# A graph network in one kernel: other program order for the first six units of its edge layer, and a last unit that ends on VectorE and ScalarE

## What is computed

```python
def _L3_gnn_ref(x, adj, W1, b1, W2, b2, gamma, beta):
    hi = jnp.einsum('bsh,hk->bsk', x, W1[:H])
    hj = jnp.einsum('bsh,hk->bsk', x, W1[H:])
    h = jax.nn.relu(hi[:, :, None, :] + hj[:, None, :, :] + b1)
    y = jnp.einsum('bijk,kl->bijl', h, W2) + b2
    y = _layernorm(y, gamma, beta)
    out = jnp.einsum('bij,bijh->bih', adj, y)
    return out
x = _layernorm(x + _L0_gnn_ref(x, adj, nodemask, ...), axis=-1)
x = _layernorm(x + _L1_gnn_ref(x, adj, adj, ...), axis=-1)
x = _layernorm(x + _L2_gnn_ref(x, adj, ...), axis=-1)
x = _layernorm(x + _L3_gnn_ref(x, adj, ...), axis=-1)
```

## Time and profile before

| | us |
|---|---|
| median of 3 runs | 465.38 (464.74 to 468.73) |
| the profiled execution | 467.42 |
| its span, first to last instruction | 465.7 |
| mean granted PE clock in it | 0.984 of full speed |
| PE busy in it | 435.3 (93%) |
| DVE, ACT, POOL busy | 411.8, 386.6, 357.8 |

### The profile page before, as it was taken

How to read it: one execution, slowest core, us unless ns; L and a number is a source line. 1 busy time by engine, 2 the same in 40 slices (tenths; PEclk the granted TensorE clock), 3 DMA queues, 4 the chain that set the end, 5 groups by cost and what they waited for, 6 DMA issues and landing times. The chain is left out here.

```text
span 465.7 us, 14118 instructions
## 1 busy us (share of the span) xinstructions
PE 435.3 (93%) x3394; PEld 414.4 (89%) x3427; DVE 411.8 (88%) x1518; ACT 386.6 (83%) x994; POOL 357.8 (77%) x656
## 2 busy tenths in 40 slices
PE   3799989999999999789999999999999999999980
PEld 2699989999999999679999999999999999999980
DVE  5799999999999999947998898899889888989873
ACT  2368979999999899787788888888888888989872
POOL 4379989998999898816777777777778776878745
PEclk9989999999999999899999999999999999999996
DMA  6134345545445652243322222222222231213111
GB/s 218 40 82 126 101 141 165 158 130 179 146 146 181 204 175 82 85 121 96 104 73 76 81 71 81 69 83 67 85 66 86 64 88 62 90 62 87 34 36 47
DMA packets 50939, 47.60 MB, mean 102 GB/s; under 512 B 5584, under 2 KB 42576, under 8 KB 50896
## 3 DMA queue, kind: packets, MB, share of 16 engines
q1 hardware_dynamic: 49600, 46.29, 32.5%
q10 hardware_dynamic: 1296, 0.83, 0.6%
HBM read 28.22 MB, written 18.87 MB: 101 GB/s over the span
## 5 line engine op out<-in xcount | busy, mean ns | idle before, releaser
L1420 PEld LDWEIGHTS bank<-w2c,hE 128*128 128x128 f32 x512 | 67.3, 192 | 2.3
L1420 PE MATMUL bank<-w2c,hE 128*128 128x128 f32 x512 | 67.5, 275 | 0.1
L833 ACT ACTIVATE hE<-bank,front 128x512 f32<-128x512 f32 x64 | 44.3, 692 | 8.6 <-PE bank L1401 8.3
L1130 DVE TENSOR_REDUCE ssum<-sqE 128x4 f32<-128x512 f32 x64 | 43.3, 677 | 7.5 <-ACT sqE L845 6.4
L845 ACT ACTIVATE sqE<-bank 128x512 f32<-128x512 f32 x64 | 38.3, 599 | 13.3 <-PE bank L1420 13.2
L999 DVE BATCH_NORM_STATS2 stats<-t 128x6 f32<-128x128 f32 x192 | 44.6, 273 | 1.2 <-issue 1.1
L1147 DVE TENSOR_TENSOR ym<-bank,wE 128x512 f32<-128x512 f32 x64 | 43.7, 683 | 1.7 <-POOL wE L680 0.4
L655 POOL TENSOR_TENSOR half<-ym 128x512 f32<-128x512 f32 x32 | 40.7, 1273 | 3.0 <-DVE ym L1147 2.6
L642 POOL TENSOR_TENSOR gHl<-gH,gHu 128x512 fp32r<-128x512 f32 x32 | 41.0, 1283 | 1.1 <-issue 1.1
L1450 PE MATMUL bank<-yC,ST 128*128 128x128 f32 x256 | 33.9, 275 | 3.1 <-DVE yC L1153 3.1
L1418 PE MATMUL bank<-bias,ones_b 128*128 128x512 bf16 x94 | 35.7, 380 | 0.1
(11 more groups left out here) (179 smaller groups left out, 1643.0 us busy)
## 6 DMA issues: line engine op xcount, KB each, us to landing
hh_scratch<-hh SPq DMA_DIRECT2D x32, 256.0 KB, 2.2
gH<-hh_scratch SPq DMA_DIRECT2D x32, 256.0 KB, 2.8
A<-adj_groups SPq DMA_DIRECT2D x32, 128.0 KB, 2.1
res_scratch<-res SPq DMA_DIRECT2D x32, 128.0 KB, 2.0
gRES<-res_scratch SPq DMA_DIRECT2D x32, 128.0 KB, 2.5
out<-y SPq DMA_DIRECT2D x32, 128.0 KB, 1.9
AT<-adjT_groups SPq DMA_DIRECT2D x30, 128.0 KB, 2.2
X<-x_groups SPq DMA_DIRECT2D x28, 128.0 KB, 2.2
```

The source lines that it names most:

```text
L833: nc.scalar.activation(hE[g][:, :], HE_ps, ACT.Relu, bias=C["L3_b1"]).then_inc(b[f"hE{g}_ready"], 1)
L1130: nc.vector.tensor_reduce(ssum[q][:, g * ELL:(g + 1) * ELL], sqE[g][:, :, :], AX.X, ALU.add).then_inc(b[f"ssE{g}_ready"], 1)
L1420: last = nc.tensor.matmul(ps[:, i, :], hidden[:, i * P:(i + 1) * P], w2c[:, :], start=False, stop=i == tiles - 1)
```

## The change

Five parts, all of order and place; what is computed stays the same.

1. A table `FIRST` with 252 moments of its own for every step of units 0 to 5 that `passage` emits; the few steps of units 6 and 7 keep the old formula. `COUNTED` becomes three moments (cast 216.47, count 216.95, full 218.74; before 217, 217.8, 218.2). SP's stages are given by the names of the steps that they follow, so that they move too. Before, `hs:0` stood at 218.8, `idx:0` at 211.0, `g0:0` at 225.8; `idx:4` at 249.2.
2. Waits that go with it: `a1` waits for `accE` of the unit before it, and `m0` of unit 0 no longer waits for `most_done`.
3. Last unit (31): VectorE does `w`, `half`, `accE`, gamma and residual instead of GpSimd; ScalarE weighs the list (`yC`) instead of VectorE; the second Square is four activations of 128 columns with an accumulating output, in place of `d1`; VectorE writes the normed output into `gRES` in place of `omean`, `oshift` and ScalarE's `y`.
4. Order at the end: `frec` of 29 and `tot` of 30 stand in front of `rec` of 31; statistics of 31 behind those of 30; `app` of 29 in front of `fstd` of 30.
5. The store of unit 30 is issued by ScalarE, that of 31 waits for `last_ready`.

```diff
+        START3, EARLY, CATCH = 216.0, 5.0, 25.0
+        FIRST = {("hs", 0): 193.88, ("hs", 1): 203.06, ("hs", 2): 228.54, ("hs", 3): 232.05, ...
...
+                 ("idx", 0): 203.62, ("idx", 1): 219.35, ("idx", 2): 223.78, ("idx", 3): 227.16, ("idx", 4): 230.38, ("idx", 5): 242.5,
+                 ("spu", 0): 204.68, ("spu", 1): 216.74, ... ("T", 0): 210.51, ... ("spl", 0): 212.12,
+                 ("spl", 1): 219.62, ... ("g0", 0): 213.17,
...
+        COUNTED = {"cast": 216.47, "count": 216.95, "full": 218.74}
+        def first_moment(when, u):
+            def of(name):
+                then = PERIOD3 / 2 * u + T3[name]
+                return FIRST.get((name, u), START3 + then - EARLY * max(0.0, 1 - then / CATCH))
+            return moment(when, of)
...
-                            then = PERIOD3 / 2 * u + at
-                            plan.append((START3 + then - EARLY * max(0.0, 1 - then / CATCH), 2, i, u, partial(stage, q, u, ...
+                            plan.append((first_moment(when, u), 2, i, u, partial(stage, q, u, ...
...
             def add_halves(q, u, count):
+                if at_end(u):
+                    return
                 pool.wait_ge(b["ymE0_ready"], count())
                 pool.wait_ge(b["ymE1_ready"], count())
+                wait_past(pool, b["accE_ready"], count(1))
...
+                    if at_end(u) and g == 1:
+                        wait_past(act, b["esd_ready"], count(2))
+                        for i in range(ELL):
+                            last = nc.scalar.activation(sqE[g][:, i, :], YE_ps[g][:, i, :], ACT.Square, accum_out=ssum[q][:, ELL + i:ELL + i + 1])
...
+                if at_end(u):
+                    act.wait_ge(b["wE_ready"], count())
...
+                    for i in range(GROUP * CSR):
+                        last = nc.scalar.activation(yC[q][:, i, :], YC_ps[:, i, :], ACT.Copy, scale=wE[q][:, 2 * ELL + i:2 * ELL + i + 1])
+                    last.then_inc(b["yC_ready"], 1)
...
             def out_std(q, u, count):
+                if isinstance(u, int) and u == UNITS - 2:
+                    apply_out(1 - q, u - 1, lambda d=0: count(d + 1))
...
             def invert(q, u, count):
+                if at_end(u):
+                    out_rstd(q, u - 2, lambda d=0: count(d + 2))
+                    total(1 - q, u - 1, lambda d=0: count(d + 1))
...
+                    nc.vector.tensor_tensor(wE[q][:, :], erstd[q][:, :], fits[:, u, :], ALU.mult).then_inc(b["wE_ready"], 1)
...
+                    if at_end(u) and g == 1:
+                        last_ends(q, u, count)
+                        total(q, u, count)
+                        last_sums(q, u, count)
...
+            def last_ends(q, u, count):
+                dve.wait_ge(b["ymE0_ready"], count())
+                dve.wait_ge(b["ymE1_ready"], count())
+                dve.wait_ge(b["accE_ready"], count(1))
+                nc.vector.tensor_tensor(half[:, :, :, :], ym[q][:, :, 0:2, :], ym[q][:, :, 2:4, :], ALU.add).then_inc(b["half_done"], 1)
+                dve.wait_ge(b["half_done"], count())
+                nc.vector.tensor_tensor(accE[q][:, :, :], half[:, :, 0, :], half[:, :, 1, :], ALU.add).then_inc(b["accE_ready"], 1)
+            def last_sums(q, u, count):
...
+                nc.vector.tensor_tensor(tot[q][:, :, :], tot[q][:, :, :], C["gamma"].unsqueeze(1).to_broadcast([P, GROUP, P]), ALU.mult).then_inc(b["gout_done"], 1)
...
+                nc.vector.tensor_tensor(gRES[q][:, :, :], tot[q][:, :, :], gRES[q][:, :, :], ALU.add).then_inc(b["tout_ready"], 1)
...
+                if at_end(u):
+                    dve.wait_ge(b["orstd_done"], count())
+                    for g in K2:
+                        last = nc.vector.tensor_scalar(gRES[q][:, g, :], gRES[q][:, g, :], omv[q][:, g, 0:1], orstd[q][:, g:g + 1], ALU.subtract, ALU.mult)
+                    last.then_inc(last_ready, 1)
...
-                        pe.wait_ge(most_done, 1)
+                        if g == 1:
+                            pe.wait_ge(most_done, 1)
```

More of the change, by code:

```diff
@@ new lines, in gnn_stack, with moment, at_end @@
+        COUNTED = {"cast": 216.47, "count": 216.95, "full": 218.74}
+        def moment(when, of=T3.get):
+            if isinstance(when, str):
+                return of(when)
+            return max(of(name) for name in when[:-1]) + when[-1]
+        def first_moment(when, u):
[3 more added lines that the diff above has]
+            return moment(when, of)
+        def at_end(u):
+            return isinstance(u, int) and u == UNITS - 1
@@ L376, in flow @@
         def flow(stages, p, counts, ages):
-            times = [(at + PERIOD3 / 2 * q, i, q) for i, (at, _) in enumerate(stages) for q in K2]
+            times = [(moment(when) + PERIOD3 / 2 * q, i, q) for i, (when, _) in enumerate(stages) for q in K2]
             for at, i, q in sorted((at % PERIOD3, i, q) for at, i, q in times):
-                age = int((stages[i][0] + PERIOD3 / 2 * q) // PERIOD3)
+                age = int((moment(stages[i][0]) + PERIOD3 / 2 * q) // PERIOD3)
                 assert age < AGES
@@ L503, in store @@
             def store(q, u, count):
-                sp.wait_ge(b["out_ready"], count())
-                sp.dma_start(out_d[bass.ds(u * GROUP, GROUP), :, :].rearrange("g p f -> p g f"), y4[q][:, :, :]).then_inc(out_stored[q], 16)
+                if isinstance(u, int) and u == UNITS - 2:
+                    return
+                if at_end(u):
+                    sp.wait_ge(last_ready, 1)
+                else:
+                    sp.wait_ge(b["out_ready"], count())
+                sp.dma_start(out_d[bass.ds(u * GROUP, GROUP), :, :].rearrange("g p f -> p g f"), (gRES if at_end(u) else y4)[q][:, :, :]).then_inc(out_stored[q], 16)
             dense_stages = [(24.2, next_a), (25.28, next_x), (25.66, next_at), (26.27, keep(ot, ot_s, "ot_ready", ot_stored)),
                      (58.51, keep(res, res_s, "res_ready", stored)), (69.62, keep(hh, hh_s, "hh_ready", stored))]
-            edge_stages = [(T3["idx"] + 0.5, next_ot), (max(T3["spl"], T3["hs"]) + 1.5, next_h), (T3["rs"] + 0.8, next_res), (T3["app"] + 1.0, store)]
+            edge_stages = [(("idx", 0.5), next_ot), (("spl", "hs", 1.5), next_h), (("rs", 0.8), next_res), (("app", 1), store)]
             rounds(sp, dense_stages)
@@ L863, in out_std, with middle_apply @@
                 nc.scalar.activation(ostd[q][:, :], omv[q][:, :, 1], ACT.Sqrt, bias=eps_col[:, 0:1]).then_inc(b["ostd_ready"], 1)
+            def middle_apply(q, u, count):
+                if not (isinstance(u, int) and u in (UNITS - 3, UNITS - 1)):
+                    apply_out(q, u, count)
             def apply_out(q, u, count):
@@ L1163, in out_stats @@
                 for g in K2:
[L1164 removed]
+                    last = nc.vector.bn_stats(ostats[q][:, g, :], (gRES if at_end(u) else tout)[q][:, g, :])
                 last.then_inc(b["ostats_done"], 1)
```

98 lines of the change are left out of this document (80 added, 18 removed), and 25 rows, old and new, of the table FIRST.

## The result

Median 462.20 us over 6 runs (461.34 to 462.88), beside 465.88 us for the kernel before in the same comparison: ratio 0.9923, 95% interval 0.9896 to 0.995, so 3.6 us less (2.3 to 4.9). A second comparison gave 462.75 against 466.18, ratio 0.992 (0.9884 to 0.9956). The time lies inside the forecast range of 457.3 to 464.4, 2.3 us above the 459.9 taken, and it is a change within 1%, where "faster by over 1%" had been given the larger chance. The profiled execution took 461.34 us, its span 459.6 us.

What follows compares the result with a forecast made beforehand. TensorE (PE) was taken as the bound. 3.5 us ahead of the loop plus 2.0 us at the end gave 5.5 us, off the median 465.38 us: 459.9 us, range 457.3 to 464.4.

Steps and rivals of the forecast that it cites:

- Passage: From dense rounds to unit loop, 188 to 216 us: unit 0's early slot work fills PE's idle time, 3.5 us gained.
- The signs named: Passage, if right: PE busy over 26 of 28 us, clock 1.00 from 194 to 198, gather before 190, no `begun` wait.
- The half-clock term: PE at reduced clock from 194 to 198 us, after idling; running at full speed there was worth 1.2 us.
- the 2.0 us for hand-overs: Up to the loop's start: small unseen waits at each hand-over of the new order, 1.2 to 2.5 us, taken as 2.0.
- 14.5 us of PE work against the 9.5 us of the dense chain: Between last `aggregate2` and last `turn3`: PE has 14.5 us of work, so the late chain of groups 28 to 31 costs nothing.
- Tail: Behind PE's last group, some 9.1 us without PE: the last unit's new end lets the store leave earlier, 2.0 us gained.
- I charge nothing: Last unit: slowing of VectorE's two-SBUF-input steps beside GpSimd priced at zero, since GpSimd has only about 1.3 us of work.
- 0.7 if all four are slow: Last unit: `half`, pair sum, gamma and residual each 1.67 times as long would cost 1.3 us, leaving 0.7 us gained.
- The tail alone gains: Rival, 22%: new PE waits before the loop eat all that the order saves; only the last unit's 2.0 us come, 463.4 us.
- Nearly all of it: Rival, 15%: 5 us ahead of the loop plus 2.5 us at the end, 457.9 us.
- The passage gains, the tail doesn't: Rival, 10%: `app:28` holds `rs:30` and both last units' statistics queue on VectorE; 461.9 us, to 461.2.
- Slower: Rival, 7%: group 27's `hh` store waits on SP behind idx 4, holding residual 31 and `w:1` on GpSimd; 469.9 us.

Runs made afterwards that it cites:

- order_only: The changed kernel with only the new order ahead of the loop; the last unit ends as in the kernel before. 462.43 us, ratio 0.9922.
- slots0: The changed kernel with new moments only for unit 0's slot steps, all other moments old, new end kept. 464.91 us, ratio 0.9979.
- tail_both: The changed kernel with unit 28's output ahead of ScalarE's list weighing and unit 31's weights ahead of frec:29 and tot:30 on VectorE. 461.33 us, ratio 0.9895.
- app_early: The changed kernel with only unit 28's normed output put ahead of the list's weighing on ScalarE. 462.23 us, ratio 0.9909.
- unit0: The changed kernel with new moments only for unit 0's slot and list steps, the other units at old moments, new end. 467.84 us, ratio 1.0033.
- units02: The changed kernel with new moments only for units 0 to 2, up to the weighted sums, new end. 468.86 us, ratio 1.0046.
- after_again: The changed kernel itself measured once more beside the kernel before. 462.75 us against 466.18, ratio 0.992.

## Why the prediction was right or wrong

**Passage: 3.5 us forecast, 3.5 to 3.9 measured** (marks of `order_only`, the repeat and after). The signs named came: over 26 us busy (27.22), clock 1.00 from 194 to 198, a slot gather at 188.17, no wait on `begun`. The half-clock term, 1.2 us, came back whole between the two profiles; in most executions of the kernel before it can hardly have been there, by the estimate above. The early `hs` and `spu` in the dense rounds were charged 0.5: the last `project1` step of PE begins 87.96 us behind the dense mark, 87.66 before, so 0.3. Of the 2.0 us for hand-overs, 0.78 us of idle time are in the passage and 0.66 more than before from 216 to 260, 1.4 together. The step that I had followed, 0.4 us in front of `g1:0`, was 0.5.

**But the reason given for it was only half of the reason.** The text counts what idles and says that slot work fills it. `slots0` fills it and gains 0.88 us. The part of the argument that carries the number, as far as these runs tell, is the other one: 14.5 us of PE work against the 9.5 us of the dense chain.

**Tail: 2.0 us forecast, 1.1 to 1.3 measured. This is the step that failed: "I charge nothing" for VectorE beside GpSimd.** `wE` took 0.5 us and `accE` 0.55 us more than alone; the text had looked at the contention, priced it at 1.3 us if everywhere, and dropped it because GpSimd had little to do. It had two steps of 0.72 us, and both fell on VectorE's critical ones, because VectorE itself wakes them: gamma of unit 30 starts right behind VectorE's `tot:30`, the residual behind `y` of 28. The list in the text, the residual, `om` and `sh` of unit 30, had left out gamma of unit 30, and `wE` was not among the four VectorE steps that it priced. The value "0.7 if all four are slow" missed to the other side. `tot:31` is 0.85 us nearer to the mark (7.01 against 7.86), forecast 1.35. From `tot` to the end 0.40 us came instead of 0.65. There VectorE ended as forecast, 3.97 us behind `tot` against 4.1, but unit 30's store, which I had called level, is issued last on ScalarE's queue (456.66) and took 2.5 us to land, against 1.8 us for unit 31's on SP. The four Squares came cheaper than my 1.35: 1.14 us from the first to the last accumulator read. With that the root (`esd`) started 2.31 us behind the mark, 2.78 before, so 0.47 us sooner than "as before", though unit 29's root stands ahead of it. This luck paid for `wE`: the weighting starts 3.84 us behind the mark, 3.67 before, where I had +0.1. The rest of the miss at `tot` lies behind the weighting, 3.17 us to `tot:31` instead of 2.7.

**Rule against row.** In the prediction the contention stood as a rule against a row, and I let the argument of little GpSimd work win. The Trainium skill, SBUF — State Buffer, section SBUF: two separate sides, is sharper than the page I had used: whichever of a GpSimd instruction that reads SBUF and a VectorE one with two SBUF inputs starts first has the port pair for its whole length, and the other blocks fully. The traces agree nearly: GpSimd's gamma ends at 449.33 and `wE` at 449.36; in `tail_both` the residual ends at 451.73 and `half` 0.55 us later, at 452.28, against 0.69 alone; and GpSimd's own `omean`, 0.20 us elsewhere, lasts 0.65 until VectorE's `half` is over. By that rule alone the charge is what is left of the first one when the second starts, 449.33 - 448.70 and 452.18 - 451.50, together 1.3 us, which would have put the tail at an estimated 0.7; the lengthening that the rows show is 0.49 + 0.55 = 1.04 us.

**The rivals.** "The tail alone gains" fell: 170.17 to 166.3. "Nearly all of it" fell too. "The passage gains, the tail doesn't" was nearer than its 10% said: `app:28` did hold `rs:30` (2.13 us of wait on `y`), and `app_early`, which takes that away, gives 0.49 us. "Slower" has the right chain and too much cover behind `residual` 31: about 1.7 us, not 4.

**The total.** 5.5 us forecast; 4.65 to 5.1 by the marks, 3.6 by the medians. 0.8 us of the difference is the tail. The rest, about 1 us between marks and medians, has no cause that these runs prove; the nearest is the term of 1.2 us for the half clock, which I read from one execution at 0.984 and took off a median of executions that mostly had 0.990 or more. I also took the profile's difference for that of the medians: start-up alone moved 3.0 us between profiles, over half of the effect.

## What to carry to other kernels

When work is moved ahead in in-order queues, idle time filled is no gain until the chain that it was waiting for has cover to its end. Move all steps of a stretch with one consistent table: both partial tables that left the kernel slower had a step waiting at the seam, and in one of them the rows point to a single scatter at its old place. A step shifted from GpSimd to VectorE is charged with the GpSimd steps that VectorE's own results release just then: put the critical one ahead of the result that wakes GpSimd. Compare profiles from a mark behind the start-up, not by their spans, and see by the mean granted clock whether the execution profiled is like most of the others.

## What the runs showed of the hardware

- VectorE with two SBUF inputs and GpSimd hardly overlap: 0.17 us becomes 0.66, 0.42 becomes 0.97, 0.69 becomes 0.93, and a GpSimd step of 0.20 becomes 0.65. Two steps of `begun`, with one full-width SBUF input, went from 0.57 to 2.12 us beside GpSimd (`unit0`). Two weighings that read PSUM stayed at 1.29 us beside it (`app_early`).
- An activation with accumulating output is two rows, the activation (0.27 to 0.29 us for 128 columns) and ACTIVATION_READ_ACCUMULATOR (0.19 to 0.22). A pair follows the next by 0.25 us, four take 1.14.
- PE's granted clock was at half for several microseconds behind idle stretches of 2.6 us (0.50 from 212 to 216 in `unit0`) and 3.75 us (0.50 from 228 to 232 in `units02`), and in the kernel before behind small waits of which the longest was 1.7 us. PE's last group of 8 matmuls took 1.16, 1.54 or 2.08 us behind the same 3.09 us of idle time (`app_early`, after, `after_again`).
- The mean granted clock of single executions of the kernel before ran from 0.979 to 0.991, and their times with it: 468.0 us in the median at 0.984 or less, 465.6 at 0.990 or more.
- A 128 KB store issued on ScalarE's queue took 2.5 us to land, one issued 0.1 us earlier on SP's 1.8.
